# First attention: the second piece of each product with v is moved half a step later

## The reference

```python
qkv = (h @ w_qkv + b_qkv).reshape(B, T, 3, NUM_HEADS, HEAD_DIM)
scores = jnp.einsum('bhqd,bhkd->bhqk', q, k) / np.sqrt(HEAD_DIM)
attn = jax.nn.softmax(scores, axis=-1)
out = jnp.einsum('bhqk,bhkd->bhqd', attn, v)
```

```python
x = x + _L0_ffn_ref(_layernorm(x, axis=-1), ...)
x = x + _L1_attn_ref(_layernorm(x, axis=-1), ...)
x = x + _L1_ffn_ref(_layernorm(x, axis=-1), ...)
```

## Time and profile before

| what | us |
|---|---|
| median of three runs | 2853.1 (2850.29 to 2854.55) |
| the profiled execution | 2849.84 |
| its span | 2848.1 |
| first attention, from its first product with v to its last | 123 to 750 |
| from the copy at 492.35 to the one at 512.58 (k = 10 to k = 2) | 20.23 |
| from the copy at 512.58 to the one at 531.48 (k = 2 to k = 10) | 18.90 |

### The profile page before, as it was taken

The page is one execution under the profiler, slowest core; times in us unless marked ns, Lnnn a source line. Parts: engine busy times, 40 slices in busy tenths (PEclk is TensorE's granted clock), DMA queues, the critical chain, the costliest instruction groups (busy, mean ns, idle before and its releaser), DMA issues.

```text
span 2848.1 us, 47438 instructions
## 1 busy us (share of the span) xinstructions
PE 2719.4 (95%) x16546; PEld 1819.9 (64%) x16546; DVE 2364.8 (83%) x3996; ACT 1997.0 (70%) x3972; POOL 1068.1 (38%) x1610
## 2 busy tenths in 40 slices
PE   4699999999999999899999999999999999999996
PEld 2122222222688888677777777777777777777774
DVE  7999999998656655777777988889888888888887
ACT  5388988888632332777777777777777777777772
POOL 4200000000300000365555656556556565565561
PEclk9699999999899999999999999999999999999998
DMA  2220000000010000000000000000000000000000
GB/s 68 89 83 24 21 17 24 24 24 2 1 60 1 1 1 1 1 1 1 1 1 1 1 1 1 1 1 3 7 1 1 1 1 8 1 1 1 1 1 16
DMA packets 31038, 35.22 MB, mean 12 GB/s; under 512 B 7656, under 2 KB 18896, under 8 KB 30672
## 3 DMA queue, kind: packets, MB, share of 16 engines
q1 hardware_dynamic: 30800, 32.18, 3.9%
HBM read 23.37 MB, written 8.39 MB: 11 GB/s over the span
## 4 chain that ended last, share of the span: by engine, by line
PE 50%; DVE 7%; issue 2%; ACT 0%; POOL 0%; POOLq 0%; DVEq 0%; ACTq 0%
PE ps L1752 8%; PE ps L1753 7%; PE ps L1757 7%; PE ps L1691 7%; PE ps L1679 7%; DVE neg_maxima L1960 3%; PE ps L1707 2%; PE ps L1709 1%; PE ps L1708 1%; PE ps L1697 1%; PE ps L1696 1%; PE ps L1695 1%; PE ps L1668 1%; PE ps L1669 1%; PE ps L1670 1%
## 5 line engine op out<-in xcount | busy, mean ns | idle before, releaser
L1960 DVE TENSOR_REDUCE neg_maxima<-ps 128x1 f32<-128x1024 f32 x512 | 624.7, 1220 | 144.8 <-PE ps L1757 141.9
L1902 ACT ACTIVATE diff_probs<-ps,neg_maxima 128x1024 f32<-128x1024 f32 x512 | 576.3, 1126 | 91.3 <-DVE neg_maxima L1960 89.4
L692 ACT ACTIVATE probs<-ps 128x512 f32<-128x512 f32 x1024 | 545.3, 600 | 123.0 <-PE ps L758 109.7
L607 DVE TENSOR_REDUCE maxima_of_halves<-ps 128x2 f32<-128x1024 f32 x512 | 586.8, 1218 | 5.4 <-PE ps L712 3.7
L1752 PE MATMUL ps<-z_T_high,y_high 128*128 128x512 f32 x1024 | 464.3, 453 | 5.6 <-ACT diff_probs L1902 5.6
L2234 POOL TENSOR_TENSOR DT_low<-DT_whole,DT_high 128x512 fp32r<-128x512 f32 x256 | 335.4, 1310 | 349.5 <-DVEq L2128 303.8
L1753 PE MATMUL ps<-z_T_low,y_high 128*128 128x512 f32 x1024 | 403.4, 394 | 0.0
L1972 DVE SCALAR_TENSOR_TENSOR D<-diff_probs,ratio 128x1024 f32<-128x1024 f32 x256 | 329.9, 1289 | 9.4 <-DVE ratio L1968 0.4
L712 PE MATMUL ps<-k_stacks,q_stacks 48*128 48x512 bf16 x1024 | 291.8, 403 | 34.4 <-DVE maxima_of_halves L607 26.3
L732 PE MATMUL ps<-probs,v_and_one 128*32 128x512 f32 (+1 forms) x3824 | 320.6, 407 | 0.0
L1757 PE MATMUL ps<-z_T_high,y_low 128*128 128x512 f32 x1024 | 318.2, 392 | 0.0
(11 more groups left out here) (304 smaller groups left out, 4964.5 us busy)
## 6 DMA issues: line engine op xcount, KB each, us to landing
q_stacks<-q_parts_dram SPq DMA_DIRECT2D x192, 32.0 KB
q_parts_dram<-qk_parts SPq DMA_DIRECT2D x12, 256.0 KB, 2.5
k_parts_dram<-qk_parts SPq DMA_DIRECT2D x12, 256.0 KB, 3.4
k_stacks<-k_parts_dram SPq DMA_DIRECT2D x32, 96.0 KB
residual<-in_L_attn_x_dram SPq DMA_DIRECT2D x4, 512.0 KB, 6.2
k_stacks<-k_parts_dram SPq DMA_DIRECT2D x32, 64.0 KB
q_stacks<-neg_max_parts SPq DMA_DIRECT2D x96, 4.0 KB, 1.7
out_dram<-residual SPq DMA_DIRECT2D x3, 512.0 KB, 3.2
```

What stands on the lines that cost most here:

```text
L607: nc.vector.tensor_reduce(mx_half[:, own, half, :, p * PB + t, :], ps[:, bank:bank + 2, :], X, ALU.max).then_inc(nat_max, 1)
L692: nc.scalar.activation(probs[:, k % PT, h, :], ps[:, (r + k + i) % S_RING, :], ACT.Exp, scale=SCALE).then_inc(s_free, 1)
L1902: nc.scalar.activation(probs[:, t % 2, m, :], ps[:, 2 * m:2 * m + 2, :].rearrange("p k n -> p (k n)"), ACT.Exp, bias=neg[:, t, m:m + 1], a ...
L1960: nc.vector.tensor_reduce(neg[:, t, m:m + 1], ps[:, 2 * m:2 * m + 2, :].rearrange("p k n -> p (k n)"), X, ALU.max, negate=True).then_inc(m ...
```

## The change

The `late` case is gone. Every product with v is now two pieces of 256 queries, at every step, and the second piece stands half a step later than before: the first piece of block k-2 behind i = 3 of step k, and the second piece of block k-3 behind i = 1 of step k. So a copy step has the last piece of the old half behind i = 1 and the first piece of the new half behind i = 3. Behind the loop one second piece is left over, and is done there.

```diff
-                        late = k % PB == LAG
...
-                            part = (True, True) if late and i == 3 else (i == 1, i == 3)
-                            if any(part) and not (late and i == 1):
-                                if k >= LAG:
-                                    products_with_v(u, r, k - LAG, *part)
-                                elif not starts(u):
-                                    products_with_v(u - 1, (r - 1) % RING, STEPS + k - LAG, *part)
+                            if i == 1 and k > LAG:
+                                products_with_v(u, r, k - 1 - LAG, False, True)
+                            elif i == 1 and not starts(u):
+                                products_with_v(u - 1, (r - 1) % RING, STEPS + k - 1 - LAG, False, True)
+                            if i == 3 and k >= LAG:
+                                products_with_v(u, r, k - LAG, True, False)
+                            elif i == 3 and not starts(u):
+                                products_with_v(u - 1, (r - 1) % RING, STEPS + k - LAG, True, False)
...
                 units(pe, unit)
+                products_with_v(UNITS - 1, (UNITS - 1) % RING, STEPS - 1 - LAG, False, True)
                 for k in range(STEPS - LAG, STEPS):
```

## The result

The changed kernel takes 2868.31 us (median of five runs, 2863.88 to 2869.34), the kernel before beside it 2850.59 (2849.76 to 2854.55): 17.7 us (0.6%) more, a ratio of 1.0057 with a 95% interval of 1.0045 to 1.0068. The profiled execution took 2869.34 us, with a span of 2867.3, against 2848.1.

A forecast was written before the change was run, and what follows sets the result against it. TensorE was taken to pace ordinary steps, and a chain through ScalarE's copy the copy steps. 29 copy steps x 0.56 + 2 x 0.59 + 0.1 = 17.5 us more, median 2870.6 us, range 2861 to 2879.

The forecast's parts named there:

- (1): Copy step, piece ahead of the transposes: halved, 0.57 us in place of 1.00, so -0.43 us each.
- (2): Copy step: ScalarE's copy must wait for the late completing piece, starting at 1.27 us instead of 0.28, +0.99 us.
- (3): Rest of the copy step's chain, copy to transposes: whole step 3.89 us against 3.33, +0.56; unit 15 +0.59.
- (4): Steps without a copy: same pieces in the same places, first and second exchanged; costed at nothing.
- (5): The ends: step k = 2 of unit 0 -0.43 us, extra piece behind the loop +0.57; together +0.1.
- Faster: ScalarE reaches the copy after the late piece is done, so only the halving counts: -8.5 us, 2844.6; chance 0.06.
- Absorbed: VectorE alone sets the pace, TensorE's delay vanishes into waits elsewhere: 2853 us or a little more; chance 0.08.
- Larger: At k = 10, VectorE tightest: another 0.5 us in 15 units, +25 us, 2878; chance 0.04.

The follow-up runs named there:

- the kernel that removes the stall: Changed kernel with ScalarE's copy moved behind the first exponential of the copy step, TensorE's queue untouched: 2848.12 us, ratio 0.9990 against the kernel before.

## Why the prediction was right, step by step

I predicted 17.5 us more; 17.7 were measured, and the interval of the ratio, 1.0045 to 1.0068, is 13 to 19 us. The median came to 2868.3 and not to 2870.6, because the kernel before had its median at 2850.6 in five runs and not at the 2853.1 of the first three. In the profiled executions the spans differ by 19.2, of which 0.9 lies ahead of the first score product (116.64 and 117.49), where the two kernels do the same; from there to the last copy it is 17.3.

**(1), the halved piece.** Predicted 0.57 in place of 1.00; the rows show 0.56 to 0.57. Right. The reading of 0.14 us as the cost "of cutting a product in two" was wrong, though it changed no term of the sum, because each piece was taken at its duration from the row. The Trainium skill, "TensorEngine Tiling (Array Packing)", section Instruction Overhead, has about 60 cycles for each matmul; the estimate from it, 0.20 us for 8 more records, is not borne out: 8 more records cost 0.00 us when the pieces stand together. I had added the 60 cycles to each record. The section itself goes on that a matmul with a free dimension of 1 takes as long as one of 60, which makes them a least length, not an addition, and with that the 0.00 agrees.

**(2), the late copy.** Predicted: the copy at 1.27 and ScalarE waiting for L732. Measured 1.25, and a bracket on each of the 31 copies in the loop. VectorE's waits at the reciprocals, 26 us expected, were 25.2. That the late copy costs by the exponential behind it is shown by the run that moved only the copy: the copy stayed as late, and all of the 17.7 us were gone.

**(3), the copy step.** Predicted 3.89, measured 3.87; each step of the chain is within 0.03. The idle 1.08 us ahead of i = 3 came to 1.27 - 0.23 = 1.04 by the starts; the bracket says 0.67, since it counts from the end of the last record. That the copy would end 0.6 us before the piece gets there was misread: by the prediction's own terms it is 0.87, and 0.87 was measured (546.71 to 547.58). Nothing hung on it. In unit 15 I had 4.06, and the rows have 4.08 (750.24 to 754.32). Predicted distances of 19.46 and 20.8 (for one that had been 20.23); measured 19.44, and 20.54 where 20.01 was the shortest before.

**(4) and (5).** Ordinary half steps stayed at 1.11 to 1.12 us (544.87 to 545.99). At the two ends I had -0.43 and +0.57. In unit 0 only 0.23 us were saved from the product of k = 2 to the step after next (4.73 us before, 4.50 after), and the piece behind the loop cost 0.43 (24 records in 2.36 us, 32 in 2.79). Together 0.2 and not 0.1. From the copy at 141.70 to the one at 732.44 it was 590.74 us before; after, from 143.29 to 751.27, 607.98: 17.24 more over 30 distances. Of these about 16.0 are the copy steps (29 x 0.53 + 0.61). The rest, 1.3 us, is in those distances that contain the shift's DMAs: counted over their shortest, they come to 1.7 us before and 3.0 after. I had not allowed for this. In the same 14 distances (up to unit 14) TensorE's waits for these DMAs sum to 1.3 us before and 2.7 after. One execution of each kernel was profiled, so this could be scatter, but the other traces speak against it: these waits are 0.5 to 1.3 us in all four kernels built on the kernel before, itself included, and 1.8 to 3.2 in all six built on the changed one, itself included. So moving the pieces seems to bring the waits with it; why was not tested. The copy steps alone come to 29 x 0.53 + 2 x 0.61 = 16.6 us, where I had 17.4, and these waits fill the gap, so that the sum came within 0.2 us is in part luck.

**The rivals.** *Faster* asked that ScalarE reach the copy later than 1.27 us; it was there 0.85 us early. Its price was mis-sized as well: the kernel that removes the stall gained 2.6 us in the medians, not the 6 I expected of it nor the 8.5 of the rival. I had added up VectorE's waits as if all could be won. From k = 2 to k = 10 VectorE has 16 maxima, one every 1.13 us, and 0.55 us for the division, 18.66 in all (the 18.20 of the earlier trace rows count the last record to its end), so that of the 18.90 only 0.24 were open; the best kernel mostly reached 18.80, and 18.71 at the shortest. *Absorbed* failed: while TensorE's chain is the longer loop, VectorE only waits elsewhere, as the transposes moved ahead show. *Larger* did not happen: at k = 10 the step grew by no more than at k = 2, and the longer waits for the shift's DMAs came to 1.3 us and not to 7.5.

## What to carry to other kernels

When a piece of work is moved later, look for the engine that waits for it, and for what is queued behind that wait: here TensorE had time for the piece, and the first exponential behind the waiting copy was what cost. If a wait has to come, put ahead of it in the queue whatever the other engine needs next. And when the stall is gone, the gain ends at the next engine's floor, which is to be read from the distances between starts in its busy stretch and not from the sum of its waits.

## What the hardware showed that I had not expected

Cutting a 512-wide product into 256-wide pieces is free if they stand together (16 records in 1.00 us, as 8 records); standing apart, between score products, each piece takes 0.57, 0.14 us more for the pair. I saw this with fp32 products in four column groups between bf16 score products, and with nothing else.
